# A pair's looked-up source rows are added to layer one behind the next chunk's look-up tiles, lane by lane

## What is computed

```python
src = src[argsort(dst)]; dst = dst[argsort(dst)]
h = jnp.maximum(_layernorm(x), 0.0)                       # 12500 x 32
e_feat = concatenate([h[src], h[dst], edge_attr_32], -1)  # 400000 x 96
hidden = relu(e_feat @ W1 + b1)                           # 400000 x 64
v = hidden @ W2 + b2                                      # 400000 x 32
x_cand = segment_max(v, dst, num_segments=12500)
out = x + maximum(x_cand, h)
```

## Time and profile before

| what | value |
|---|---|
| time, median of 3 runs | 3183.11 us |
| span of the profiled execution | 4798.8 us |
| mean granted clock of PE in it | 0.832 |
| PE busy (matmul) | 3796.5 us, 79% |
| PE weight loads | 2547.3 us, 53% |
| DVE busy | 2178.1 us, 45% |
| ACT busy | 2192.4 us, 46% |
| POOL busy | 2386.6 us, 50% |
| chain that ended last | PE 60%, issue 19%, DVE 8%, ACT 2% |

### The profile page before, as it was taken

How to read it: one execution, slowest core, us unless ns; L and a number is a source line. 1 busy time by engine, 2 the same in 40 slices (tenths; PEclk the granted TensorE clock), 3 DMA queues, 4 the chain that set the end, 5 groups by cost and what they waited for, 6 DMA issues and landing times.

```text
span 4798.8 us, 56874 instructions
## 1 busy us (share of the span) xinstructions
PE 3796.5 (79%) x19778; PEld 2547.3 (53%) x19778; DVE 2178.1 (45%) x2474; ACT 2192.4 (46%) x2555; POOL 2386.6 (50%) x2523
## 2 busy tenths in 40 slices
PE   5858788778878877877887788778877887778787
PEld 3536455555555545555555555555555555555465
DVE  4211554445444444544444455444444454445356
ACT  2214454445444444544444445444544454445355
POOL 6653455555455455455545555555455555554310
PEclk8979888888778888888887888888888888888798
DMA  8700222222222222222222222222222222222112
GB/s 255 279 10 25 70 80 88 92 85 61 57 68 63 56 66 69 56 61 68 68 55 63 68 65 61 60 69 68 56 63 68 69 61 56 68 68 68 46 55 56
DMA packets 200553, 350.32 MB, mean 73 GB/s; under 512 B 73791, under 2 KB 124251, under 8 KB 200117
## 3 DMA queue, kind: packets, MB, share of 16 engines
q1 hardware_dynamic: 116638, 303.65, 18.4%
q0 software_dynamic: 80448, 41.33, 6.2%
q10 hardware_dynamic: 3332, 4.01, 0.3%
HBM read 240.36 MB, written 119.78 MB: 75 GB/s over the span
## 4 chain that ended last, share of the span: by engine, by line
PE 60%; issue 19%; another core or an unknown queue 10%; DVE 8%; ACT 2%; DMA 0%; DVEq 0%; ACTq 0%; SPq 0%
PE ps_rows L938 38%; PE ps_layers L968 8%; PE ps_layers L963 5%; DVE onehot L1250 3%; PE ps_layers L918 2%; PE ps_layers L953 2%; PE ps_layers L912 2%; DVE max_t L1318 2%; PE ps_layers L957 2%; PE ps_layers L1006 1%; DVE src_t L1285 1%; DVE rows_in L1323 1%; ACT onehot L852 0%; DVE dst_t L1305 0%
## 5 line engine op out<-in xcount | busy, mean ns | idle before, releaser
L664 POOL DMA_INDIRECT src_in<-h_dram,src_ix x2269 | 2147.7, 947 | 1951.5 <-PE ps_rows L938 976.5
L938 PE MATMUL ps_rows<-onehot,table 128*128 128x512 f32 x9898 | 2553.2, 418 | 109.0 <-issue 89.3
L938 PEld LDWEIGHTS ps_rows<-onehot,table 128*128 128x128 f32 x9898 | 1986.6, 203 | 728.8 <-issue 292.8
L852 ACT ACTIVATE onehot<-distance 128x1024 fp32r<-128x1024 bf16 x909 | 905.0, 1049 | 855.0 <-PE ps_rows L938 607.3
L847 ACT ACTIVATE distance<-picks,below_column 128x1024 bf16<-128x1024 int16 x909 | 985.1, 1139 | 0.7 <-DMA picks<-picks_dram 0.7
L838 ACT ACTIVATE hid<-ps_layers,b_col 128x512 f32<-128x512 f32 (+1 forms) x404 | 241.6, 680 | 1407.9 <-remote 912.0
L1300 DVE STREAM_TRANSPOSE ps_layers<-rows_in 128x512 f32<-128x512 f32 x202 | 133.3, 706 | 1561.3 <-ACT hid L838 1561.2
L968 PE MATMUL ps_layers<-picked_rows,w_src 128*64 128x128 f32 x1552 | 399.9, 390 | 550.1 <-issue 545.7
L1250 DVE SCALAR_TENSOR_TENSOR onehot<-picks,column,ps_layers 128x1024 fp32r<-128x1024 int16 x404 | 499.8, 1258 | 310.2 <-PE ps_rows L938 164.7
L968 PEld LDWEIGHTS ps_layers<-picked_rows,w_src 128*64 128x64 f32 x1552 | 188.8, 180 | 784.9 <-issue 782.2
L1318 DVE TENSOR_TENSOR_SCAN max_t<-mask_in,max_t,ps_layers 128x512 f32<-128x512 bf16 x196 | 249.0, 1271 | 337.2 <-remote 331.4
(11 more groups left out here) (145 smaller groups left out, 1283.1 us busy)
## 6 DMA issues: line engine op xcount, KB each, us to landing
picks<-picks_dram SPq DMA_DIRECT2D x101, 512.0 KB
first_rows<-hid SPq DMA_DIRECT2D x100, 500.0 KB
rows_in<-in_edge_attr_dram SPq DMA_DIRECT2D x96, 512.0 KB
rows_in<-first_rows SPq DMA_DIRECT2D x96, 512.0 KB
run_max<-rows_in SPq DMA_DIRECT2D x96, 512.0 KB
src_in<-h_dram,src_ix POOLq DMA_INDIRECT x2269
mask_in<-mask_dram SPq DMA_DIRECT2D x96, 256.0 KB
h_dram<-h_sb ACTq DMA_DIRECT2D x4, 392.0 KB, 5.9
```

What stands on the lines that cost most here:

```text
L664: pool.indirect_dma_start(out=src_in[:, slot, g, r, :], out_offset=None, in_=rows[:, :], in_offset=bass.IndirectOffsetOnAxis(ap=src_ix[:, ...
L852: nc.scalar.activation(onehot[:, RING_AT[c] + BY_DVE[c] + k, :, :].rearrange("p g w -> p (g w)"), distance[:, k, :], ACT.Relu, bias=1.0, s ...
L938: mm = nc.tensor.matmul(ps_rows[g][side][:, 0:WIDE], table[:, i * SIDES + side, part, :], onehot[:, RING_AT[c] + t, g, :], start=(i + part ...
```

## The change

The four lanes' L968 matmuls are taken out of `layer_one` into a function `add_picked`, one lane a call, and `look_up` of chunk 0 calls it behind each of its four tiles, after the tile's semaphore step. Arithmetic, operands and PSUM banks stay as they are. The minis keep their order.

```diff
+assert CHUNK[0] == A
@@ look_up
-            def look_up(j, slot, c):
+            def look_up(j, slot, c, behind_tile=None):
...
                     mm.then_inc(tiles_used, 1)
+                    if behind_tile is not None:
+                        behind_tile(t)
@@ layer_one
+            def add_picked(j, slot, a, short=False):
+                gathered = [GATHERED, SHORT_GATHERED if short else GATHERED]
                 pe.wait_ge(rows_masked, j * MASKS + MASKS)
-                for a in range(A):
-                    for g in range(2):
-                        mm = nc.tensor.matmul(ps_hid[a][g * HID:(g + 1) * HID, gathered[g]:gathered[g] + PICKED], w_src[:, :],
-                                              picked_rows[:, slot, g, a * PICKED:(a + 1) * PICKED], start=False, stop=True)
-                    mm.then_inc(hid_summed, 1)
+                for g in range(2):
+                    mm = nc.tensor.matmul(ps_hid[a][g * HID:(g + 1) * HID, gathered[g]:gathered[g] + PICKED], w_src[:, :],
+                                          picked_rows[:, slot, g, a * PICKED:(a + 1) * PICKED], start=False, stop=True)
+                mm.then_inc(hid_summed, 1)
@@ pair
                 if mini:
                     layer_one_mini(j, slot, True)
+                    look_up(j + 2, slot, 0)
                 else:
                     layer_one(j, slot, True, short)
-                look_up(j + 2, slot, 0)
+                    look_up(j + 2, slot, 0, lambda t: add_picked(j, slot, t, short))
```

## The result

The changed kernel takes 3335.14 us (median of 4 runs, 3333.59 to 3341.67), the kernel before in the same comparison 3181.96 us (4 runs, 3179.34 to 3183.89). The ratio is 1.0484, with a 95% interval of 1.0472 to 1.0496: slower by 153 us. The forecast was 3405 us, range 3290 to 3475. Sign and range held; the likeliest case's own range, 3370 to 3450, did not, and the loss is 70 us smaller than the sum said.

The account below looks back on a forecast made before the run. PE was taken as the bound, at 27.28 us a pair. Changeovers +1.11, the relu wait +0.90 and DVE's chain +0.29 gave +2.30 us x 97 = +223 us on 3183: 3406, forecast as 3405 us, range 3290 to 3475.

Parts of the forecast that it names:

- the likeliest case: Whole kernel: PE's turn grows from 27.28 to 29.58 us, giving 3405 us, own range 3370 to 3450; chance 0.58.
- the wait for the last lane: PE ahead of layer two waits for ACT's relu of lane 3 (L838): +0.90 us a pair, bounds 0.67 and 1.2.
- The changeovers: PE in chunk 0, switching between look-up tiles and L968's lanes: 9.62 us against 8.51, +1.11 us a pair.
- dearer ends: Switching ends twice as dear: chunk 0 with lanes 10.0 to 11.1 us; with DVE falling behind, 3440 to 3500, chance 0.08.
- DVE behind it: DVE's chain from fill_dst starts only with layer two, making L953 late: +0.29 us a pair, bounds 0 and 0.9.
- the row of the short pair: Near the end, chunk 0 takes 7.56 us after 0.47 us idle, so short stops keep the clock: 3406 us.
- the 2.4 us a pair of the rival: PE's stops lower its clock, chunk 0 taking 9.92 us instead of 7.49 every pair: 3639 us, chance 0.04.
- +2.30 us x 97: PE's added time a turn, 29.58 against 27.28 us, paid in 96 full pairs and the short one: +223 us.
- the clean pair: Pair near the end of the first trace, L968 at 1.02 us: 27.28 us, taken as the timed run's turn.
- the timed pair is not PE's 27.28 us: Loop pair up to 28.35 us, held by gathers or a starved L968: 3302 to 3406, middle 3350, chance 0.15.
- starving of L968: PE's L968 matmuls 0.7 us apart amid the profiled loop; in the timed run at most 1.07 us a pair.
- POOL is given more time; nothing: POOL issues 24 gathers a pair and gets more time in the longer turn; costed at nothing.

Follow-up runs that it names:

- half of the gathers: Every second gather in the loop replaced by a copy of one row: kernel before 3137.95 us (ratio 0.9865), changed kernel 3333.00 us (ratio 1.0469).

## Why the prediction was right, and where its size was off

**The turn.** The forecast was 29.58 us for 27.28; measured 29.57 for 27.27. Its terms: the wait for the last lane +0.90, measured 0.88, in the whole 85.4 us, and the kernel with only the last lane behind a tile shows it alone. The changeovers +1.11, measured 1.33: from the start of the gathered source rows to layer two without the wait, 2419.01 to 2430.51 less 0.88 is 10.62 us, before 2922.99 to 2932.28, 9.29. A lane of 0.37 and a tile of 2.04 are what the sum had (0.37 and 2.04); what it missed is 0.12 over the chunk (9.74 us for 9.62), 0.07 of it behind the last lane, and 0.09 between L966 and the first tile. (The lower bound for dearer ends, 10.0, was not worked out: twice the ends of the lanes alone makes 10.2.) DVE behind it +0.29, measured 0.11 (L1012 to L956 16.33 us for 16.22): DVE's chain started with layer two as said, after 8.81 us of waiting for the last relu, but ran 0.10 us faster from there to L1275, so the room of 4.5 us was used up almost exactly. L956 waits for one-hots only ten times, 18.2 us in all, 3.7 of them behind 1100 us. The errors in these two terms cancel, which is luck. Luck it is too that the range held: the 3335 us are the time of a rival with a chance of 0.15, not of the likeliest case.

**The clock.** The granted clock is 1.00 from 790 us to the loop's end, the 2.4 GHz level, and 0.993 over the span, though PE now stops for 0.88 us in each turn. So the row of the short pair decided rightly, and the 2.4 us a pair of the rival did not come. The Trainium skill (Perfetto Trace Analysis, Matmul Optimizations) says that the matmul engine scales its power with its use. Stops of 0.88 us show nothing of that in this trace. The windows of after, over the same three stretches of turns:

```profile
364.00:790.00 426.00, 403.72 (x2500) 282.86 (x2508) 289.81 (x303) 290.52 (x310) 313.96 (x333) 0.99 0.35 117
790.00:2566.00 1776.00, 1716.57 (x10688) 1208.12 (x10680) 1226.46 (x1262) 1251.74 (x1321) 1342.41 (x1423) 1.00 0.33 94
2566.00:3217.00 651.00, 629.09 (x3924) 442.72 (x3909) 448.21 (x462) 458.55 (x484) 451.16 (x478) 1.00 0.31 90
```

Long stops are another matter. In the turn of 46.91 us of before, PE stopped for 12.27 us and ran behind it at a mean granted clock of 0.76, then stopped for 4.17 us and ran at 0.66:

```profile
2684.00:2698.00 14.00, 12.65 (x42) 9.86 (x42) 9.13 (x9) 0.00 (x0) 10.65 (x12) 0.76 0.35 114
2701.00:2706.00 5.00, 4.37 (x56) 1.87 (x58) 4.84 (x7) 5.00 (x7) 3.78 (x5) 0.66 0.41 150
```

The 42 look-ups take 12.65 us there and would take 9.75 by the prediction's 0.227 us each and 0.22 for the ends, so a small part of what before loses in its late turns is clock.

**The step that failed: "+2.30 us x 97".** It took the clean pair for every pair of before. 96 x 2.26 would be 217 us; the three stretches give 9.2, 131.4 and 10.0, 151 in all.
- Late turns: 50 expected, 10 measured. Before loses 41 us there to the supply of gathers, after nothing. This is shown: with half of the gathers the loss is gone from before, after is unchanged, and the distance is 195 us.
- First 14 turns: 32 expected, 9 measured. All kernels take 29 to 30 us a turn there, the orders differ by little, and half of the gathers gives before 7 us. In that stretch picks come late (ACT waits 74.0 us for them in before, 55.5 in after) and the one-hots with them (PE waits 30.3 and 14.5 us); what makes the picks late (copies that fill the maxima run there) wasn't tried and stays open.
- The middle: 136 expected, 131 measured; every 14 pairs before loses 0.3 to 4.1 us over its clean turns, after 0.2 to 1.7; why wasn't tried.

**Where it could have been seen.** The rebuild from the clean pair came out at 3230 us, 47 too much, and I put that ahead of the loop. The loop really begins at 365 us, not 496, so the part ahead is 131 us shorter than in that trace, and the clean pair then makes the loop too short by 83: 365 + 96 x 27.28 + 115 is 3099. With PE's 345.6 us of work as a bound I had written that the pair could be up to 28.35 us; the true mean is (3067.2 - 365.5) / 96 = 28.14. That is the rival "the timed pair is not PE's 27.28 us", held by gathers, at 3302 to 3406 with a middle of 3350; 3335 is its time, and its cause is half right (gathers late in the loop, not starving of L968). It had 0.15 and should have had more: 24 gathers a pair were in the text, their 1.25 us each could be read from the first trace too (its gathers at 2501.69 and 2502.94 us, say), and 30.0 against 27.3 says that they can't keep up. "POOL is given more time; nothing" was the sentence to stop at: an engine that the change gives more time is a gain somewhere if it was short of it.

## What to carry to other kernels

Before a difference per turn is multiplied by the turns, set each engine's own supply per turn beside the bound's, also of an engine that runs ahead: POOL at 70 to 75% busy issued without a pause, 30.0 us a pair against PE's 27.3, and only its lead hid it. Then a dearer turn is partly absorbed (here 42 of 195 us), and by the same working, which no run here tried, a cheaper one would gain nothing once the lead is used up. Work that another engine must answer goes at least that answer's time (0.88 us for a relu of 128x512) ahead of the instruction that needs it, and small matmuls of another shape go in one block: every block more cost 0.37 us a turn.

## What was not expected of the hardware

- One profiled execution took 4798.8 us where the same program took 3181.8 profiled again: a trace can be of a run that no timed one is like. Its clean stretches still gave the right turn.
- A gather of 128 rows costs POOL 0.944 us and 0.30 us between two, 1.25 us in all, in every kernel here that gathers all rows. A copy of one row in a gather's place still takes POOL 0.535 us (233.7 us for 437 of them), with next to no gap: from 1000 to 2000 us of before POOL is busy for 756 us with 802 gathers, and for 662 with 437 gathers and as many copies.
- Each block of picked rows more between the 128x128 look-ups lengthens the turn by 0.37 to 0.39 us, with two lanes in it as with four (28.05 us with two blocks of two, 27.65 with one of four, 27.27 before). The blocks themselves last 0.37, 0.59 and 1.02 us with one, two and four lanes, about 0.11 us a step.
